# A fused attention and expert block on one core: the order of ScalarE and VectorE, in the loop and in the drain

## Chip, cores and metric

One core of one Trainium2 chip runs the whole program. The metric is the device time of one execution in microseconds (us). Its engines are TensorE (PE), VectorE (DVE), ScalarE (ACT), GpSimd (POOL) and SyncE (SP, which here only issues DMAs); each runs its own list of instructions in order and waits for the others by semaphores.

## What is computed

x has 16 images of 256 rows and 128 channels. Six rows of modulation per image come from a small matmul. Cut to what matters:

```python
h = layernorm(x) * (1 + ca) + sa
wave = silu(h @ wave_w.T + wave_b)           # 8 frequencies, 8 phases
freq, phase = mean(sigmoid(wave[0]) * 15 + 1), mean(tanh(wave[1]) * 16)
w = silu(h @ kernel_w.T + kernel_b)[..., :33]          # per head
pos = clip(l + (s - 16) * freq + phase, 0, 255)        # 33 places per row
out = sum_s w[s] * lerp(h, pos[s])                     # per head of 16 channels
x = x + ga * silu(out @ out_w.T)
h = layernorm(x) * (1 + cb) + sb
mask = one_hot(top_2(softmax(h @ router_w.T + router_b)))   # 8 experts
x = x + gb * (sum_e mask[e] * (h @ expert_w[e]) + mask @ expert_b)
```

## The kernel before

The 16 images are handled in nine units: image 0 alone, seven pairs, image 15 alone (`UNITS`, `LATE` is unit 7, `LAST` unit 8). An image is two tiles of 128 rows. The order of each engine is written out by hand as one loop over i, in which `run(i, lag, stage)` issues `stage` for unit i + lag, and `second` does so for the second image of a pair. So one iteration works on several units at once: the front of unit i + 1 (norm, transposes, projection rows, the line of positions), the middle of unit i (network, AT, A, attention), the back of unit i - 1 (sum with x, second norm, logits, the two best experts) and the experts of unit i - 2. What follows the loop is the drain.

The middle, on VectorE: `network` (L814, six stages of predicated copies that move the 33 weights of each row to their places in T, masks from `eI`), `spread_out` (L847, AT from T and the cells c, one instruction for each tile), `set_ends` (L857). `places` (L770) makes `eI` of unit i + 1 from uR, which ScalarE makes in `front_u` (L484, L491). On ScalarE, `front_c` (L502) and `front_fall` (L508, the Relu) make c, and `mid_A` (L519) copies A out of four PSUM banks, which TensorE fills with transposes (L1066, `mid_A`). `mid_attend` (L1080), `mid_y` (L1090) and `mid_gate` (L1096) end in pY.

The back: `residual` (L866, VectorE) adds pY to x and leaves row sums. ScalarE's `stats2` (`squares`, L380 and L383) and GpSimd's `rstd2` (L322, L328, L330) give the norm, `norm2` (L417) applies it, TensorE transposes xn (`back_x2T`, L1106), ScalarE makes h2T (`back_h2T`, L552), TensorE the logits (`back_logits`, L1117), VectorE `lg`, `top` and `hit` (L880 to L896), TensorE and ScalarE the mask rows mkT (`back_mk`, L1127 and L561). SyncE writes mkT to DRAM (L297) and reads it back to all partitions as mkb (L301, `masks`). In the next iteration VectorE's `masked` (L915) multiplies mkb and h2T into hm for each image, TensorE runs a plain part and seven experts for each image (`back_plain` L1167 and L1170, `back_experts` L1151), ScalarE scales (`back_moe`, L568), TensorE transposes back (L1177), and `total` (L920) adds to x. Units 7 and 8 spread their masks by TensorE instead (`back_mb`, L1139, read by `masked` at L909).

The sums for the first norm of unit i + 2 are `sums1` (L394), `squares1` (L383) and `norm1` (L417) on ScalarE, `rstd1` on GpSimd. `warm_up` (L1000) issues matmuls whose result nobody reads. ScalarE's order in the part of the loop that the change touches:

```python
run(i, 1, front_row, 2)
run(i, 0, front_fall)
run(i, 1, front_row, 3)
run(i, 1, front_wave)
...
run(i, -1, stats2)
...
run(i, 2, sums1)
run(i, 1, front_u)
run(i, -1, norm2)
...
run(i, 2, squares1)
run(i, -1, back_h2T)
run(i, -2, back_moe)
run(i, 0, mid_A, 0)
run(i, -1, back_mk)
```

## Time and profile before

| | |
|---|---|
| runs shown | 292.1, 292.21, 293.36 us; median 292.21 |
| the profiled execution | 291.6 us, its span 289.8 us |
| PE busy | 263.6 us (91%) |
| DVE busy | 259.2 us (89%) |
| ACT busy | 228.0 us (79%) |
| POOL busy | 40.2 us (14%) |
| network of unit 8 starts (end of the loop) | 242.71 us |

The span is the time from the first to the last instruction of the profiled execution. In the views below times are in us from the start of the span; a timeline row gives start, length and the instruction (line, operation, output from inputs, count), and in brackets how long the engine had been idle before it and what it waited for. Rows that start where the one before them still has its last tenth of a us overlap it. A table by stage has, for each engine, its busy time and the number of instructions, then the clock granted to TensorE (1.00 is 2.4 GHz, 0.50 is 1.2 GHz).

### The profile page before, as it was taken

The numbers are of one execution on the slowest core, as the hardware profiler recorded it, in microseconds if no ns is written. First come the engines' busy times: TensorE is split into PE (matmuls) and PEld (weight loads), VectorE is DVE, ScalarE is ACT, GpSimd is POOL, SyncE is SP. The second block draws the span as 40 slices with busy tenths as digits, with TensorE's granted clock in tenths as the row PEclk, the third lists the DMA queues.
The fourth block names the chain that finished last, engine by engine and source line by source line (L and its number), as shares of the span: only waits on it lengthen the run. The fifth ranks groups of instructions, "written<-read, shape, count | busy, mean of one in ns | idle before, by whom it ended". The sixth has DMA issues, their size and how long they took to land.

```text
span 289.8 us, 5448 instructions
## 1 busy us (share of the span) xinstructions
PE 263.6 (91%) x1884; PEld 182.7 (63%) x1884; DVE 259.2 (89%) x543; ACT 228.0 (79%) x641; POOL 40.2 (14%) x61
## 2 busy tenths in 40 slices
PE   7999886999889998999899998999999989999895
PEld 3444642874567476866587477837884778487664
DVE  7989999998969998999989998999999999973462
ACT  4885899599978998899979998899779767655310
POOL 4203402300410022000200012002400300040100
PEclk9999998699999999999999999999999999999999
DMA  6550000020002000050005000500041004100101
GB/s 180 195 129 0 0 0 0 2 66 1 1 0 119 31 1 0 3 163 3 0 1 165 0 0 2 160 8 1 2 104 62 1 0 118 49 2 0 38 0 54
DMA packets 11869, 12.08 MB, mean 42 GB/s; under 512 B 1014, under 2 KB 10818, under 8 KB 11842
## 3 DMA queue, kind: packets, MB, share of 16 engines
q1 hardware_dynamic: 11398, 11.33, 13.0%
q10 hardware_dynamic: 444, 0.40, 0.5%
q8 instruction: 15, 0.25, 0.3%
q14 instruction: 12, 0.10, 0.1%
HBM read 9.59 MB, written 2.14 MB: 40 GB/s over the span
## 4 chain that ended last, share of the span: by engine, by line
ACT 32%; DVE 31%; PE 24%; issue 11%; POOL 1%; ACTq 0%; DVEq 0%; POOLq 0%
DVE AT L847 13%; ACT A L519 6%; DVE T L814 5%; ACT xn L383 4%; PE pT L1066 4%; ACT xn L417 4%; ACT c L502 3%; PE pE L1151 3%; PE pY L1151 2%; PE pL L1117 2%; PE pR L1066 2%; ACT u L484 2%; ACT T L453 2%; ACT hT L440 2%; PE pR L1043 1%
## 5 line engine op out<-in xcount | busy, mean ns | idle before, releaser
L814 DVE COPY_PREDICATED T<-mask,T 128x1472 f32<-128x1472 int16 (+9 forms) x54 | 76.6, 1418 | 0.5
L847 DVE TENSOR_TENSOR AT<-T,c 128x2064 f32<-128x2064 f32 x32 | 72.4, 2305 | 0.0
L519 ACT ACTIVATE A<-pT 128x512 f32<-128x512 f32 x64 | 35.1, 603 | 27.6 <-PE pT L1066 27.0
L1151 PE MATMUL pE<-hm,late 128*128 128x256 f32 x196 | 47.0, 387 | 0.0
L1151 PEld LDWEIGHTS pE<-hm,late 128*128 128x128 f32 x196 | 35.8, 190 | 5.9
L1066 PE MATMUL pT<-first,AT 128*128 128x128 f32 x256 | 34.6, 279 | 3.2 <-DVE AT L857 3.1
L519 ACT ACTIVATE A<-pR 128x512 f32<-128x512 f32 x64 | 35.5, 622 | 0.3 <-PE pR L1066 0.3
L322 POOL TENSOR_SCALAR ve<-sq 128x4 f32<-128x4 f32 (+1 forms) x14 | 9.9, 710 | 185.3 <-ACT xn L383 185.3
L1066 PEld LDWEIGHTS pT<-first,AT 128*128 128x128 f32 x256 | 29.4, 144 | 9.2 <-DVE AT L857 7.7
L1066 PE MATMUL pR<-first,AT 128*128 128x128 f32 x256 | 33.9, 276 | 0.0
L1080 PE MATMUL pY<-A,hs 128*32 128x256 f32 x512 | 32.4, 383 | 0.3
L1066 PEld LDWEIGHTS pR<-first,AT 128*128 128x128 f32 x256 | 29.8, 144 | 0.0
L417 ACT ACTIVATE xn<-x,nm,rs 128x128 f32<-128x128 f32 x64 | 26.4, 483 | 2.2 <-POOL nm L330 2.2
L915 DVE TENSOR_TENSOR hm<-mkb,h2T 128x1792 f32<-128x1792 bf16 x13 | 26.2, 2017 | 1.2 <-POOL rs L328 1.2
L502 ACT ACTIVATE c<-near,early 128x172 f32<-128x172 f32 (+1 forms) x54 | 26.0, 569 | 0.0
L1043 PE MATMUL pR<-proj,hT 128*128 128x297 f32 x62 | 23.8, 465 | 0.9 <-ACT hT L440 0.9
L328 POOL TENSOR_TENSOR rs<-ve,mhalf 128x4 f32<-128x4 f32 (+1 forms) x18 | 17.4, 968 | 42.3 <-DVE ve L727 35.4
L1080 PEld LDWEIGHTS pY<-A,hs 128*32 128x32 f32 x512 | 16.9, 109 | 9.5 <-ACT A L519 4.9
L1000 PE MATMUL pE<-warm 128*128 128x512 bf16 x88 | 21.3, 400 | 1.2 <-DVE warm L655 1.2
L383 ACT ACTIVATE xn<-x,mu 128x128 f32<-128x128 f32 x52 | 20.2, 390 | 0.5
L1000 PE MATMUL pT<-warm 128*128 128x512 bf16 x65 | 18.1, 401 | 0.0
L1000 PEld LDWEIGHTS pE<-warm 128*128 128x128 bf16 x88 | 8.9, 103 | 11.5 <-issue 1.9
(153 smaller groups left out, 403.1 us busy)
## 6 DMA issues: line engine op xcount, KB each, us to landing
mkb<-mask_rows SPq DMA_DIRECT2D x6, 896.0 KB, 5.0
x<-in_x SPq DMA_DIRECT2D x7, 256.0 KB, 5.7
out<-x SPq DMA_DIRECT2D x7, 256.0 KB, 5.0
late<-in_late SPq DMA_DIRECT2D x1, 592.0 KB, 3.8
mkb<-mask_rows SPq DMA_DIRECT2D x1, 448.0 KB, 3.5
x<-in_x SPq DMA_DIRECT2D x2, 128.0 KB, 3.5
wmod<-in_wmod ACTq DMA_DIRECT2D x1, 256.0 KB, 4.4
out<-x SPq DMA_DIRECT2D x2, 128.0 KB, 3.2
```

Source lines behind the costliest of these rows:

```text
L383: ins = nc.scalar.activation(junk[:, bt, :], of_x(n)[:, bt, :], ACT.Square, bias=mu[:, bt:bt + 1], accum_out=sq[:, bt:bt + 1])
L417: ins = nc.scalar.activation(xn[:, bt, :], of_x(n)[:, bt, :], ACT.Identity, bias=nm[:, bt:bt + 1], scale=rs[:, bt:bt + 1])
L502: nc.scalar.activation(cells[:, :, :, r], near[:, 0:w, :], ACT.Abs, bias=off[:, r:r + 1]).then_inc(a_abs, 1)
L519: nc.scalar.activation(A[b][:, m, 2 * j:2 * j + 2, :].rearrange("p h l -> p (h l)"), four_banks(k)[:, :], ACT.Copy).then_inc(a_A, 1)
L814: nc.vector.copy_predicated(rows[:, :, :, j0:j1], spread(mask[:, k, 0:w, j0:j1], [P, w, H, j1 - j0], 2), rows[:, :, :, j0 + (1 << bit):j1 ...
L847: nc.vector.tensor_tensor(cells_of(bt).rearrange("p h (j r) -> p h j r", r=BLK), spread(T[n % 2][:, bt, 0:H, 0:NB], [P, H, NB, BLK], 3), s ...
L915: nc.vector.tensor_tensor(hm[b][:, :, :], mkb[n % 2][:, :, b * L:(b + 1) * L], spread(own, [P, EM, L], 1), ALU.mult).then_inc(v_hm, 1)
L1000: mm(bank[:, :], warm[:, 0:P], warm[:, :], start=True, stop=True)
L1043: mm(dst, hT[:, bt * P:(bt + 1) * P], proj[:, :], start=False, stop=True).then_inc(t_row, 1)
L1066: ins = nc.tensor.transpose(four_banks(k)[:, c0:c0 + P], AT[:, 2 * b + i, 2 * j + a, OVER + m * P:OVER + (m + 1) * P], ident)
L1080: ins = mm(pY[32 * j:32 * j + 32, b * L:(b + 1) * L], hs[n % 2][:, 2 * b + m, hh, :], A[b][:, m, hh, :], start=(m == 0 and a == 0), stop=( ...
L1151: ins = mm(dst, weT[:, e, :], hm[b][:, e, :], start=False, stop=(e == EM - 1))
```

## The change

ScalarE: `front_fall` moves behind `stats2`; `norm2` moves ahead of `sums1`, and `back_h2T` ahead of `front_u`. VectorE: from iteration 3 on the sum with x (`residual`) stands behind the second masked input; `selectors` moves to the end of iteration 0's network; `expert_weights` moves there from GpSimd, one iteration later; in the drain both masked inputs of unit 6 stand among the stages of unit 8's network. SyncE: the last mkb transfer is issued in two parts with a semaphore each. TensorE: `back_plain` covers both images in one pass; in iteration i the transposes of xn stand behind two of the seven experts of the second image; the four warm-ups behind them are issued in iterations 1 and 2 alone; in iteration 7 `back_mk(6)` stands between the halves of A; the drain runs unit 6's experts before unit 8's A.

```diff
@@ sync, masks(n)
-                sp.dma_start(mkb[n % 2][:, :, 0:w], spread(scratch[n % 2][:, 0:w], [P, EM, w], 0)).then_inc(d_mkb[n % 2], 16)
+                parts = ((0, L, d_mkb[n % 2]), (L, w, d_mkl)) if n == LATE - 1 else ((0, w, d_mkb[n % 2]),)
+                for c0, c1, landed in parts:
+                    sp.dma_start(mkb[n % 2][:, :, c0:c1],
+                                 spread(scratch[n % 2][:, c0:c1], [P, EM, c1 - c0], 0)).then_inc(landed, 16)
@@ gpsimd
-            def expert_weights():
-                pool.wait_ge(d_late, 32)
-                nc.gpsimd.tensor_tensor(weT[:, 0:EM, :], weT[:, 0:EM, :], spread(weT[:, EM, :], [P, EM, C], 1),
-                                        ALU.subtract).then_inc(g_we, 1)
-                pool.wait_ge(g_we, 1)
-                nc.gpsimd.tensor_scalar(weT[:, EM, :], weT[:, EM, :], 2.0, None, ALU.mult).then_inc(g_we, 1)
...
-                if i == 0:
-                    expert_weights()
@@ scalar, loop
                 run(i, 1, front_row, 2)
-                run(i, 0, front_fall)
                 run(i, 1, front_row, 3)
                 run(i, 1, front_wave)
...
                 run(i, -1, stats2)
+                run(i, 0, front_fall)
                 if i >= 0:
                     run(i, 1, front_hs)
+                run(i, -1, norm2)
                 run(i, 2, sums1)
+                run(i, -1, back_h2T)
                 run(i, 1, front_u)
-                run(i, -1, norm2)
...
                 run(i, 2, squares1)
-                run(i, -1, back_h2T)
                 run(i, -2, back_moe)
-                run(i, 0, mid_A, 0)
-                run(i, -1, back_mk)
+                run(i, 0, mid_A, 0, (0,))
+                if i == LATE:
+                    back_mk(LATE - 1)
+                run(i, 0, mid_A, 0, (1,))
+                if i < LATE:
+                    run(i, -1, back_mk)
@@ scalar, drain
             mid_gate(LATE)
+            back_moe(LATE - 1)
             mid_A(LAST, 0)
...
             back_mk(LATE)
-            back_moe(LATE - 1)
@@ vector
+            def expert_weights():
+                dve.wait_ge(d_late, 32)
+                (the two operations as above, on nc.vector, with v_we)
...
                 run(i, 0, network, range(4, 5))
-                run(i, -1, residual)
+                if i < 3:
+                    run(i, -1, residual)
                 second(i, -2, masked, 1)
+                if i >= 3:
+                    run(i, -1, residual)
                 run(i, 0, network, range(5, 6))
+                if i == 0:
+                    selectors()
+                elif i == 1:
+                    expert_weights()
@@ vector, drain
-            network(LAST, range(2, 6))
             masked(LATE - 1, 0)
+            network(LAST, range(2, 4))
+            masked(LATE - 1, 1)
+            network(LAST, range(4, 6))
...
             stats2(LATE)
-            dve.wait_ge(g_rs2, LATE + 1)
-            masked(LATE - 1, 1)
             route(LATE)
             residual(LAST)
             stats2(LAST)
+            total(LATE - 1)
             masked(LATE, 0)
-            total(LATE - 1)
@@ tensor
-                mm(dst, weT[:, EM, :], h2T_of(n)[:, b * L:(b + 1) * L], start=True, stop=False)
+                w = tiles(n) * P
+                mm(moe_bank(n)[:, 0:w], weT[:, EM, :], h2T_of(n)[:, 0:w], start=True, stop=False)
...
                 run(i, -2, back_experts, 0)
-                second(i, -2, back_experts, 1)
+                second(i, -2, back_experts, 1, range(0, 2))
...
                 run(i, -1, back_x2T)
-                if i > 0:
+                second(i, -2, back_experts, 1, range(2, EM))
+                if 0 < i < 3:
                     warm_up(4, pT[0])
...
+                if i == LATE:
+                    back_mk(LATE - 1)
                 run(i, 0, mid_A, 0, 1)
-                run(i, -1, back_mk)
+                if i < LATE:
+                    run(i, -1, back_mk)
@@ tensor, drain
-            warm_up(5, pT[0])
+            back_experts(LATE - 1, 0, range(0, 4))
             mid_y(LATE)
-            warm_up(6, pT[0])
-            back_experts(LATE - 1, 0, range(0, 2))
+            back_experts(LATE - 1, 0, range(4, EM))
             mid_gate(LATE)
-            back_experts(LATE - 1, 0, range(2, EM))
+            back_experts(LATE - 1, 1)
+            warm_up(8, pT[0])
             mid_A(LAST, 0, 0)
             mid_A(LAST, 0, 1)
+            back_out(LATE - 1)
...
             mid_gate(LAST)
-            back_experts(LATE - 1, 1, range(3, 6))
+            warm_up(4, pT[0])
             back_mk(LATE)
-            back_experts(LATE - 1, 1, range(6, EM))
             back_mb(LATE, 0)
-            back_out(LATE - 1)
             back_experts(LATE, 0, range(0, 4))
```

## Rows read from the trace of the kernel before

**Rows 1.** The page, busy time and share of the span.
```profile
PE 263.6 (91%) x1884; PEld 182.7 (63%) x1884; DVE 259.2 (89%) x543; ACT 228.0 (79%) x641; POOL 40.2 (14%) x61
```
**Rows 2.** Busy time by stage: iteration 5, iteration 7, the drain.
```profile
153.16:184.13 30.97, 28.66 (x221) 21.00 (x219) 29.81 (x57) 28.44 (x82) 3.13 (x6) 1.00 0.14 39
...
214.09:242.71 28.62, 26.72 (x211) 19.65 (x209) 28.38 (x58) 22.14 (x56) 2.22 (x3) 1.00 0.15 42
242.71:289.80 47.09, 42.72 (x294) 30.50 (x291) 28.59 (x79) 20.22 (x46) 3.93 (x4) 1.00 0.14 40
```
**Rows 3.** Timeline of VectorE, the waits in iterations 0, 2, 3 and 5.
```profile
20.87 0.22 DVE L735 TENSOR_REDUCE sums<-th 128x8 f32<-128x64 f32 x1 [0.70 <-ACT th L475]
...
83.73 0.19 DVE L880 TENSOR_TENSOR lg<-pL,rb 128x32 f32<-128x32 f32 x1 [2.83 <-PE pL L1117]
...
114.70 0.19 DVE L880 TENSOR_TENSOR lg<-pL,rb 128x32 f32<-128x32 f32 x1 [1.15 <-PE pL L1117]
...
176.64 0.19 DVE L880 TENSOR_TENSOR lg<-pL,rb 128x32 f32<-128x32 f32 x1 [0.92 <-PE pL L1117]
```
**Rows 4.** Timeline of VectorE, iteration 0 and one masked input of iteration 5.
```profile
29.79 2.27 DVE L801 TENSOR_TENSOR near<-sf,f 128x172 f32<-128x172 f32 x1
...
32.94 1.07 DVE L674 CAST sel<-first 24x896 bf16<-24x896 f32 x1
...
159.77 2.01 DVE L915 TENSOR_TENSOR hm<-mkb,h2T 128x1792 f32<-128x1792 bf16 x1
```
**Rows 5.** Timeline of GpSimd: the expert weights, and two last steps of a norm.
```profile
29.77 2.09 POOL L356 TENSOR_TENSOR late<-late 128x896 f32<-128x896 f32 x1
...
76.89 1.33 POOL L330 TENSOR_TENSOR nm<-mu,rs 128x4 f32<-128x4 f32 x1
...
200.62 0.77 POOL L330 TENSOR_TENSOR nm<-mu,rs 128x4 f32<-128x4 f32 x1
```
**Rows 6.** Timeline of TensorE and VectorE in iteration 1: y's transposes, the sum with x.
```profile
39.52 0.44 PE L1096 MATMUL pY<-first,y 128*128 128x128 f32 x2 [0.36 <-ACT y L541]
...
42.27 0.27 DVE L866 SCALAR_TENSOR_TENSOR x<-pY,x 128x128 f32<-128x128 f32 x1
```
**Rows 7.** Timeline of TensorE: pauses for xn, experts of an image, hT's transposes.
```profile
48.33 0.44 PE L1106 MATMUL pX<-first,xn 128*128 128x128 f32 x2 [2.19 <-ACT xn L417]
...
79.95 0.66 PE L1106 MATMUL pX<-first,xn 128*128 128x128 f32 x4 [1.50 <-ACT xn L417]
...
165.81 3.29 PE L1151 MATMUL pE<-hm,late 128*128 128x256 f32 x14
...
223.52 0.38 PE L1049 MATMUL pX<-first,hT 128*128 128x128 f32 x2
```
**Rows 8.** Busy time and granted clock behind the pause at 46 us.
```profile
49.00:55.00 6.00, 5.83 (x23) 4.04 (x22) 6.00 (x16) 2.70 (x9) 2.84 (x3) 0.50 0.01 3
```
**Rows 9.** Timeline of ScalarE in iteration 5: Relu, stats2, sums1, u, norm2, h2T.
```profile
164.23 1.05 ACT L508 ACTIVATE c<-c 128x1032 f32<-128x1032 f32 x1
...
166.07 0.19 ACT L380 ACTIVATE mu<-sum 128x4 f32<-128x4 f32 x1
...
168.32 0.30 ACT L394 ACTIVATE xn<-x 128x128 f32<-128x128 f32 x1
...
169.49 1.38 ACT L484 ACTIVATE u<-early,nlf,invf 128x50 f32<-128x50 f32 x4
...
171.18 1.63 ACT L417 ACTIVATE xn<-x,nm,rs 128x128 f32<-128x128 f32 x4
...
174.49 1.00 ACT L552 ACTIVATE h2T<-pX,modT 128x256 f32<-128x256 f32 x2
```
**Rows 10.** Timeline of VectorE: AT in iteration 2, prodN in iteration 6.
```profile
75.86 4.52 DVE L847 TENSOR_TENSOR AT<-T,c 128x2064 f32<-128x2064 f32 x2
...
200.53 0.79 DVE L825 TENSOR_TENSOR prodN<-T,kap 128x608 f32<-128x608 f32 x1
```
**Rows 11.** The page, DMA issues: count, KB each, median us to landing.
```profile
mkb<-mask_rows SPq DMA_DIRECT2D x6, 896.0 KB, 5.0
```

50 lines of the change are left out of this document (26 added, 24 removed).

## Prediction

> **What bounds the kernel now.** The page first: VectorE and TensorE are both busy for about nine tenths of the span, ScalarE for four fifths [rows 1]. Busy time by stage comes next. In a full iteration of the loop (153.16 to 184.13) VectorE works 29.81 of 30.97 us, ScalarE 28.44 and TensorE 28.66: VectorE leads, and ScalarE has some 2.5 us of room. In the drain VectorE is busy for 30.5 of 47.1 us and TensorE for 42.7 [rows 2]. So the loop goes by VectorE, the drain by TensorE. The timeline of VectorE then shows where it stands still in the loop: 0.70 us in iteration 0 for the tanh of the next unit, and at the logits 2.83, 1.15, 0.92 (two such) us in iterations 2 to 5 [rows 3]. Those waits, 5.8 us in all, are what the new order of ScalarE can win.
>
> I write T for the start of an iteration's network: 153.16 for iteration 5 [rows 2], so its 176.64 is T+23.5.
>
> **The start: expert weights and selectors.** Removed from GpSimd: two instructions. The first, 2.09 us long, started 0.02 us before VectorE's `near`, which took 2.27 us where its sisters take about 0.34 [rows 4, 5]; removing it gives back 1.93 us. They come to VectorE as a product-like operation of 896 elements (half of the 1792 that take 2.01 us, so 1.0 us [rows 4]) and a small one of some 0.2 us: +1.2 us, nothing beside it to hide it. The selectors (1.07 us [rows 4]) only move; they now stand where VectorE waited 0.70 us, so that wait goes: -0.7. But everything behind them in iteration 0, AT's first half too, is 0.3 us later, and with it the chain through A, y and its transposes (39.52 to 39.96), while the sum with x (42.27) would come 2.6 us earlier, at 39.6 [rows 6]. It then waits until 40.3: +0.65. Net at the end of iteration 1: -0.7 - 1.93 + 1.2 + 0.65 = **-0.8 us**.
>
> **Iteration 1, TensorE's pause.** Before, TensorE paused 2.19 us for xn, and right after it the granted clock stood at 0.50, the 1.2 GHz level, for 6 us and more [rows 7, 8]. In the new order xn(0) is ready about 1.7 us earlier (norm2 ahead of sums1 and u), while the 18 warm-ups still run, so that pause goes. What TensorE has after it (four and two warm-ups, four logits matmuls) ends near 48.9, and A's transposes can't start before VectorE's first ends, about 51.4. The pause is 2.5 us and lies later: the low clock would now fall on both halves of A and on the attention. With no low clock the next chain starts as soon as AT is there, and iteration 2 ends 1.3 us earlier than before; with the low stretch of before (6.8 us, half of it lost) it ends 1.3 us later. I take half such a stretch, since the work behind this pause is dense: **-0.4 us** at the start of iteration 3, ends -1.3 and +1.3.
>
> **Iteration 2.** Here ScalarE is the bound before and after. stats2 comes 1.0 us earlier, since the Relu (1.05 us [rows 9]) stands behind it; norm2, sums1, h2T and then u follow. GpSimd's last step ran into AT: 1.33 us against its usual 0.20, ending with the AT instruction [rows 5, 10]. It does so again, so norm2 starts at AT's first end in any case. The logits are 1.4 us earlier, but u is now behind h2T and `places` (eI from uR), which stands before the logits on VectorE and before the ends that release A, waits 3.4 us instead. So the 2.83 us become a wait in another place, and only what the chain gained is left; that is inside the -0.4.
>
> **Iterations 3 to 5.** The sum with x stands behind the second masked input (2.01 us, 1.94 from start to start) and ends at T+13.0. ScalarE, which started stats2 at T+12.9 [rows 9], is there earlier, now that the Relu is behind, but waits for the sum: stats2 at T+13.1, ending T+14.9. GpSimd needs three steps, the last at T+16.5. VectorE's prodN starts at T+16.4. In iteration 6 of before the same order of starts (200.62 behind 200.53) cost it 0.77 us instead of 0.20 [rows 5, 10]. The Trainium skill, "SBUF — State Buffer", section "SBUF: two separate sides", says that GpSimd and VectorE share a pair of ports as an exclusive lock, held for a whole instruction. By that rule the step waits in every iteration from three on, as the row has it. So norm2 starts at T+17.35 and ends T+18.9 (its four take 1.63 us, the last 0.09 beside the next); sums1 takes 1.17, h2T 0.9, u with uR 1.69 [rows 9]: uR at T+22.7. VectorE asks for it at T+21.95: a wait of 0.75. TensorE, with 14 passes of 3.29 us for each half [rows 7] and two of seven experts ahead of xn's transposes, has the logits at T+22.7, ahead of the question. The question for the logits moves from T+22.55 to T+23.25, against T+23.7, T+23.5 and T+23.5 of before [rows 3]: **-1.0 us** for the three. Iteration 6 had no wait; with two tiles less in sums1 the new one is 0.3: **+0.3**.
>
> What is queued behind the new waits: `set_ends` and the second half of AT on VectorE; behind stats2 on ScalarE the Relu, done at T+15.9, which AT doesn't need before prodN and prodF are done, past T+17. mkT comes 1.0 us later against T, and mkb's transfer (5.0 us at the median [rows 11]) lands at about T+5.3, 1.3 us ahead of its first reader; one slow transfer of 6.6 us would cost 0.5. The four warm-ups removed, and `back_plain` in one pass of 512 columns instead of two of 256, save TensorE 1.2 us an iteration, beside other work: nothing.
>
> **Iteration 7.** The next unit has one image, so TensorE is at the experts 2.3 us sooner in the iteration (hT's transposes at T+9.4 [rows 7], T being 214.09 [rows 2]). Plain part 1.2, first half 3.1, two experts 0.9: done at 229.2. xn(6) comes from the sum (now 227.1), 1.8 of stats2, 1.8 of GpSimd, 1.5 of norm2: 232.4. The other five experts (2.2 us) and the logits come after it: logits at 236.25, asked for at 235.7. VectorE waits 0.55 and TensorE enters the drain 0.8 later: **+0.8 us**.
>
> **The drain.** TensorE's work is nearly the same: 12 warm-ups instead of 11 (+0.2), three double passes merged (-0.7). New pauses: before the logits of unit 7 (0.6, no expert work is left to fill it), before its masks (0.9 in two); gone: 0.7 at the masks, where ScalarE's copy waited for the experts. VectorE has the masked inputs 3 us ahead of TensorE. AT of the last unit comes 2.4 us later but 2 us before TensorE is free of the experts and 8 warm-ups. Splitting mkb's transfer adds one issue, with slack. Sum: **-0.1 us**.
>
> **Sum.** -0.4 - 1.0 + 0.3 + 0.8 - 0.1 = -0.4 us. The profiled execution took 291.6 us (span 289.8 and 1.8 around it), so 291.2; the median of the runs is 0.6 above the profiled one, which gives 291.8.
>
> **Rivals.**
> *A. The low clock in iteration 7 (slower).* The pause of TensorE between the second expert and xn's transposes is 3.2 us there. A pause of 2.19 was followed by the low clock, one of 1.50 was not [rows 7, 8]. If it decides, ten us of unbroken TensorE work behind it run partly at 1.2 GHz, and the drain behind them is TensorE's too, so each microsecond lost counts: 1.7 us for half a stretch, 3.4 for a whole one. That is 293.5 to 295.2. For it: the length. Against: dense matmuls on both sides of the pause, where before, warm-ups with gaps and tiny matmuls followed. Chance 0.29; it decides above about 2 us of pause.
> *B. No low clock anywhere and GpSimd gets in ahead of prodN (faster).* 0.1 us earlier is enough for that. Then norm2 starts 0.7 earlier, the waits for uR and the logits vanish in iterations 3 to 6 (-3.0 in place of -0.7) and the start keeps -1.3; iteration 7 loses 0.5: -1.3 - 3.0 + 0.5 - 0.1 = -3.9, or 288.3. For it: in iterations 3 to 5 of before VectorE lost 3.0 us at the logits, and 1 us less in front of them is in reach. Against: the sum with x is itself 1.9 us later. Chance 0.27.
> *C. The forecast*, new waits about as long as the old: 0.44.
>
> **Range and chances.** 289.0 leaves out the best half of B; 294.9 takes in most of A. A measurement of this kernel tells 0.5% (1.5 us) from no change, so faster is below 290.75: most of B and the lower edge of C (only the better end of iteration 1 moves it there), 0.35. Slower is above 293.67: most of A, 0.23. Same: 0.42.
>
> **What the profile would show.** Right: `near` in iteration 0 at 0.34 us; no wait for th in iteration 0; VectorE waiting for ScalarE's uR at `places`, 3 us in iteration 2 and under 1 in 3 to 5, and hardly at the logits; GpSimd's last step at 0.7 us or more; an idle TensorE before xn's transposes, 1.5 us in 3 to 6 and 3 in 7; a drain of 47 us. Wrong: no wait at `places`; a granted clock of 0.5 anywhere behind iteration 3; a masked input waiting for mkb; or a drain more than 1 us longer or shorter.

## The result: slower by 3.8%, and the profile after

The changed kernel took 303.95 us in the median of six runs (301.88 to 307.56), the kernel before 292.15 us in its six beside them (291.55 to 293.46). The ratio is **1.038, interval 1.033 to 1.043**. The forecast was 291.8 in a range of 289.0 to 294.9; the result lies 9 us above the range. Executions over 1.5% longer than the shortest one of the same kernel, like the one of 307.56 us, count in no ratio. The profiled execution took 304.53 us with a span of 302.70.

The page of the changed kernel, its busy line and two costly groups (GpSimd's, and the norm on ScalarE with its idle time and what ended it):

```profile
PE 265.7 (88%) x1844; PEld 181.9 (60%) x1844; DVE 258.8 (86%) x545; ACT 228.9 (76%) x641; POOL 65.7 (22%) x59
...
L332 POOL TENSOR_TENSOR rs<-ve,mhalf 128x4 f32<-128x4 f32 (+1 forms) x18 | 33.8, 1879 | 48.6 <-DVE ve L733 41.8
L410 ACT ACTIVATE xn<-x,nm,rs 128x128 f32<-128x128 f32 x64 | 26.7, 490 | 21.8 <-POOL nm L334 21.8
```

Against [rows 1] VectorE, ScalarE and TensorE did as much as before. GpSimd is the one that changed: 65.7 us instead of 40.2, with fewer instructions, and ScalarE waited 21.8 us for GpSimd's last step of a norm. In the page of before those two groups stood like this:

```profile
L417 ACT ACTIVATE xn<-x,nm,rs 128x128 f32<-128x128 f32 x64 | 26.4, 483 | 2.2 <-POOL nm L330 2.2
...
L328 POOL TENSOR_TENSOR rs<-ve,mhalf 128x4 f32<-128x4 f32 (+1 forms) x18 | 17.4, 968 | 42.3 <-DVE ve L727 35.4
```

The same 18 steps of four numbers per partition (the power -1/2) took 968 ns each before and 1879 ns after. Nothing in the change touches them. Busy time by stage, as [rows 2], for iterations 4, 5, 7 and the drain:

```profile
125.06:158.41 33.35, 28.61 (x213) 19.66 (x212) 29.80 (x58) 28.25 (x82) 9.92 (x7) 1.00 0.12 37
158.41:192.78 34.37, 29.51 (x213) 21.44 (x212) 29.90 (x57) 28.95 (x84) 10.17 (x8) 0.95 0.11 35
...
223.23:253.82 30.59, 26.53 (x200) 19.31 (x199) 28.53 (x57) 22.60 (x58) 1.43 (x3) 0.94 0.16 48
253.82:302.70 48.88, 42.90 (x291) 30.43 (x290) 28.40 (x79) 20.20 (x46) 2.10 (x4) 1.00 0.12 34
```

VectorE works 29.8 us in a full iteration as before; the iteration lasts 33.35 us instead of 30.97. The fifth number pair is GpSimd: 9.92 us instead of 3.13. The granted clock (the third number from the right) was 1.00 there, so it is not TensorE's clock that makes iteration 4 longer. So the time went into waits. The list of VectorE's waits names them (us in total, times, the longest), first of the changed kernel, then of before, which has no wait for uR:

```profile
DVE eI L776 <- ACT uR L484: 14.0, 6, 3.5
DVE lg L886 <- PE pL L1132: 11.0, 3, 8.7
```
```profile
DVE lg L880 <- PE pL L1117: 10.9, 5, 5.1
```

The 8.7 and the 5.1 us stand in the drain. In the loop the waits for the logits did shrink, from 5.8 to 2.3 us, as the change meant them to.

The starts of the iterations, read as T was read in the prediction (the first network stage on VectorE's timeline), give a table that every run below is compared by (profiled executions, us):

| kernel | start of it. 2 | it. 2 | it. 3 to 5 | it. 6 | it. 7 | drain |
|---|---|---|---|---|---|---|
| before | 58.66 | 32.30 | 93.17 | 29.96 | 28.62 | 47.09 |
| changed | 57.88 | 33.76 | 101.14 | 30.45 | 30.59 | 48.88 |
| difference | -0.78 | +1.46 | **+7.97** | +0.49 | +1.97 | +1.79 |

The differences add up to 12.9 us, the growth of the span (302.7 - 289.8). Eight of them lie in three iterations that the forecast had at -1.0. Iteration 5 is 1.0 us longer than iteration 4 and has a granted clock of 0.95 in the table by stage, some 3.4 us at the 1.2 GHz level; that part may be the clock's.

**How an iteration loses 2.4 us.** First GpSimd's timeline, from iteration 3 into 4 of the changed kernel. Steps ve, rs, nm come in threes; the first three are those of the first norm of unit i+2, the others (their ve is left out) of the second norm of unit i-1, one iteration on.

```profile
118.92 0.19 POOL L326 TENSOR_SCALAR ve<-sq 128x4 f32<-128x4 f32 x1 [7.37 <-ACT xn L376]
119.19 6.13 POOL L332 TENSOR_TENSOR rs<-ve,mhalf 128x4 f32<-128x4 f32 x1
125.40 0.21 POOL L334 TENSOR_TENSOR nm<-mu,rs 128x4 f32<-128x4 f32 x1
...
141.62 1.46 POOL L332 TENSOR_TENSOR rs<-ve,mhalf 128x4 f32<-128x4 f32 x1
143.16 1.74 POOL L334 TENSOR_TENSOR nm<-mu,rs 128x4 f32<-128x4 f32 x1
```

Then VectorE's timeline over the same time:

```profile
117.02 0.37 DVE L776 SCALAR_TENSOR_TENSOR eI<-uR,early 128x200 int16<-128x200 f32 x1 [3.31 <-ACT uR L484]
...
119.16 0.31 DVE L798 SCALAR_TENSOR_TENSOR sf<-sc,u 128x172 f32<-128x172 f32 x1
119.40 0.35 DVE L902 TENSOR_TENSOR hit<-late,topi 128x192 bf16<-128x192 f32 x1
119.67 4.51 DVE L853 TENSOR_TENSOR AT<-T,c 128x2064 f32<-128x2064 f32 x2
124.10 0.33 DVE L807 TENSOR_TENSOR near<-sf,f 128x172 f32<-128x172 f32 x1
124.35 0.21 DVE L863 COPY AT<-endw 128x32 f32<-128x32 f32 x1
```

And ScalarE's, which stands behind both:

```profile
125.73 1.65 ACT L410 ACTIVATE xn<-x,nm,rs 128x128 f32<-128x128 f32 x4 [1.97 <-POOL nm L334]
...
139.32 0.19 ACT L373 ACTIVATE mu<-sum 128x4 f32<-128x4 f32 x1
...
144.93 1.65 ACT L410 ACTIVATE xn<-x,nm,rs 128x128 f32<-128x128 f32 x4 [2.31 <-POOL nm L334]
```

1. The power step is asked for at 119.19, 0.03 us behind the start of sf. It is recorded until 125.32. Its unheld length is 1.01 us, so its own work began at about 124.31, as near gave way to the copy of the ends. All of VectorE's instructions between 119.16 and that point read two operands in SBUF.
2. The first norm of the next unit waits 1.97 us for it on ScalarE, in the next iteration, and everything behind it there is late: stats2 starts at T+14.26 (139.32 - 125.06). The sum with x had ended at T+13.0 (138.05), as forecast.
3. The second norm's steps therefore come a microsecond later than the forecast had them and meet prodN (141.42) and the first half of AT (142.54 to about 144.8). norm2 starts at T+19.87, not T+17.35; uR is 2.5 us late, and VectorE waits 3.31 us at `places`, not 0.75.
4. VectorE's later half of the iteration moves, but ScalarE's squares1 moves too, and asks for the power step 0.03 us behind sf again: 152.54 6.13 us in iteration 4. The loop holds itself there.

Before, the first norm's steps were asked for at T+21.6 (174.75), as VectorE's first pair of AT ended (175.20). Behind it VectorE ran small instructions or stood, and the steps took 0.51, 1.01 and 0.20 us:

```profile
174.75 0.51 POOL L322 TENSOR_SCALAR ve<-sq 128x4 f32<-128x4 f32 x1 [5.07 <-ACT xn L383]
175.33 1.01 POOL L328 TENSOR_TENSOR rs<-ve,mhalf 128x4 f32<-128x4 f32 x1
176.42 0.20 POOL L330 TENSOR_TENSOR nm<-mu,rs 128x4 f32<-128x4 f32 x1
```

squares1 then stood ahead of h2T; the change put it last, behind norm2, sums1, h2T and u, at T+27.

### The profile page after: what moved, and what is told of

Read it like the earlier page. It is cut to its first block, busy times and chain, and to the rows that moved or that the text cites. A ratio compares the mean times of both kernels' runs of the same rounds, so it can differ in the third digit from the quotient of the medians.

```text
span 302.7 us, 5384 instructions
## 1 busy us (share of the span) xinstructions
PE 265.7 (88%) x1844; PEld 181.9 (60%) x1844; DVE 258.8 (86%) x545; ACT 228.9 (76%) x641; POOL 65.7 (22%) x59
## 4 chain that ended last, share of the span: by engine, by line
ACT 34%; PE 23%; DVE 17%; POOL 14%; issue 10%; ACTq 0%; POOLq 0%; DVEq 0%
POOL rs L332 9%; ACT A L512 9%; ACT xn L410 6%; ACT xn L376 5%; POOL nm L334 4%; DVE T L820 4%; PE pE L1168 4%; DVE AT L853 4%; PE pT L1081 3%; ACT c L495 3%; PE pR L1058 2%; PE pY L1168 2%; ACT u L477 2%; ACT y L534 2%; PE pR L1081 2%
## 5 line engine op out<-in xcount | busy, mean ns | idle before, releaser
L1168 PE MATMUL pE<-hm,late 128*128 128x256 f32 x196 | 48.1, 397 | 0.0
L332 POOL TENSOR_TENSOR rs<-ve,mhalf 128x4 f32<-128x4 f32 (+1 forms) x18 | 33.8, 1879 | 48.6 <-DVE ve L733 41.8
L410 ACT ACTIVATE xn<-x,nm,rs 128x128 f32<-128x128 f32 x64 | 26.7, 490 | 21.8 <-POOL nm L334 21.8
L326 POOL TENSOR_SCALAR ve<-sq 128x4 f32<-128x4 f32 (+1 forms) x14 | 5.9, 421 | 167.8 <-ACT xn L376 167.8
L1168 PEld LDWEIGHTS pE<-hm,late 128*128 128x128 f32 x196 | 37.9, 200 | 7.0 <-issue 1.8
L1081 PE MATMUL pT<-first,AT 128*128 128x128 f32 x256 | 37.1, 291 | 5.2 <-DVE AT L863 5.0
L1081 PEld LDWEIGHTS pT<-first,AT 128*128 128x128 f32 x256 | 30.3, 149 | 12.6 <-DVE AT L863 10.4
L1081 PE MATMUL pR<-first,AT 128*128 128x128 f32 x256 | 35.7, 285 | 0.0
L334 POOL TENSOR_TENSOR nm<-mu,rs 128x4 f32<-128x4 f32 (+1 forms) x18 | 23.8, 1321 | 1.4
L1095 PEld LDWEIGHTS pY<-A,hs 128*32 128x32 f32 x512 | 15.9, 109 | 12.4 <-ACT A L512 7.4
L1015 PE MATMUL pE<-warm 128*128 128x512 bf16 x88 | 21.8, 405 | 1.2 <-DVE warm L652 1.2
L1121 PE MATMUL pX<-first,xn 128*128 128x128 f32 x32 | 6.3, 324 | 13.6 <-ACT xn L410 13.5
```

The costliest lines, as they stand in the source:

```text
L332: nc.gpsimd.tensor_tensor(rs[:, 0:w], ve[:, 0:w], mhalf[:, 0:w], ALU.pow).then_inc(out, 1)
L334: nc.gpsimd.tensor_tensor(nm[:, 0:w], mu[:, 0:w], rs[:, 0:w], ALU.mult).then_inc(last, 1)
L410: ins = nc.scalar.activation(xn[:, bt, :], of_x(n)[:, bt, :], ACT.Identity, bias=nm[:, bt:bt + 1], scale=rs[:, bt:bt + 1])
L1081: ins = nc.tensor.transpose(four_banks(k)[:, c0:c0 + P], AT[:, 2 * b + i, 2 * j + a, OVER + m * P:OVER + (m + 1) * P], ident)
L1095: ins = mm(pY[32 * j:32 * j + 32, b * L:(b + 1) * L], hs[n % 2][:, 2 * b + m, hh, :], A[b][:, m, hh, :], start=(m == 0 and a == 0), stop=( ...
L1168: ins = mm(moe_bank(n)[:, b * L:(b + 1) * L], weT[:, e, :], hm[b][:, e, :], start=False, stop=(e == EM - 1 and b == UNITS[n][1] - 1))
```

## The experiments

### Which part of the change costs what

**Runs e6 and e7**: the kernel before with one part of the change each.

```diff
# e6: ScalarE's loop order alone (stats2, Relu, hs, norm2, sums1, h2T, u, squares1)
# e7: the sum with x behind the second masked input from iteration 3 on, alone
-                run(i, -1, residual)
+                if i < 3:
+                    run(i, -1, residual)
                 second(i, -2, masked, 1)
+                if i >= 3:
+                    run(i, -1, residual)
```

> The kernel before with ScalarE's new order in the loop alone (Relu behind stats2, norm2 ahead of sums1, h2T ahead of u, squares1 last). Theory L2 (squares1 now ends so late that GpSimd's steps of the first norm meet the second pair of AT instructions and end after both, so the next iteration's xn is late on ScalarE): the pow step takes 6 us in iterations 2 to 5, periods rise to 31.5 us or more, and the kernel is 1 to 3% slower than before although the sum with x has not moved: 295 to 300 us. Rival M (only the moved sum does harm, the order alone wins the logits' waits): 287 to 290 us.

> The kernel before with the sum with x behind the second masked input from iteration three on, nothing else. By now theory L2 says that the first norm's steps on GpSimd decide and the second norm's hardly: ScalarE has u ahead of norm2 here, norm2 starts at T+18.0, and GpSimd's last step ends by T+17.3 even if held off by prodN. So no change: 291 to 293 us, wait at the logits 1.0 to 1.4 us in iterations 3 to 5. Theory L as first stated (the moved sum decides) expects at least 2 us more per iteration, 298 or above.

e6: 300.28 us, ratio **1.032 (1.028 to 1.036)**. e7: 292.38 us, 1.001 (0.998 to 1.004). ScalarE's order alone makes most of the loss; the later sum alone is worth nothing in the whole (its iterations 3 to 5 took 94.5 us against 93.2, its iteration 2 0.6 us less). GpSimd's timeline of e6 shows why, and which of the two norms does it:

```profile
117.51 6.12 POOL L328 TENSOR_TENSOR rs<-ve,mhalf 128x4 f32<-128x4 f32 x1
...
139.98 1.01 POOL L328 TENSOR_TENSOR rs<-ve,mhalf 128x4 f32<-128x4 f32 x1
141.06 0.20 POOL L330 TENSOR_TENSOR nm<-mu,rs 128x4 f32<-128x4 f32 x1
```

The second norm's steps are as quick as they can be. The first norm's power step takes 6.1 us, and iterations 2 to 6 last 31.8, 33.0, 32.7, 32.7 and 32.7 us.

**Runs e1 and e2**: the changed kernel with one part undone each (e1 ScalarE's old loop order, e2 the sum with x first in every iteration).

```diff
# e1, ScalarE
                 run(i, 1, front_row, 2)
+                run(i, 0, front_fall)
...
                 run(i, -1, stats2)
-                run(i, 0, front_fall)
...
-                run(i, -1, norm2)
                 run(i, 2, sums1)
-                run(i, -1, back_h2T)
                 run(i, 1, front_u)
+                run(i, -1, norm2)
...
                 run(i, 2, squares1)
+                run(i, -1, back_h2T)
# e2, VectorE
-                if i < 3:
-                    run(i, -1, residual)
+                run(i, -1, residual)
                 second(i, -2, masked, 1)
-                if i >= 3:
-                    run(i, -1, residual)
```

> The changed kernel with ScalarE's old order in the loop (the Relu ahead of the last row, u ahead of norm2, h2T behind squares1); all else as changed. Theory L (GpSimd's last step of the second norm is held off by VectorE's long two-input instructions, because the sum with x now comes 1.9 us later): norm2 still can't start before AT's first instruction ends, so the loss stays and only moves from the wait for uR to the logits: 300 to 305 us, 2 to 3 us of wait at the logits in iterations 3 to 5. Rival O (the new order itself costs it: u stands behind norm2, sums1 and h2T whatever GpSimd does): the loss goes, 291 to 294 us.

> The changed kernel with the sum with x ahead of the second masked input in every iteration. Theory L: stats2 ends a microsecond or more sooner, GpSimd's last step starts ahead of prodN and takes 0.2 us; the wait for uR in iterations 3 to 5 falls from 3.3 us to under 0.5 and the time to 291 to 296 us. Rival O: the sum is not what decides; the waits for uR stay above 2 us and the time at 300 us or more.

e1: 298.08 us, 1.018 (1.013 to 1.024). With the old order no power step of the loop took over 1.43 us from iteration 1 on; iterations 3 to 5 took 95.1 us. VectorE waited for the logits in their place, 19.0 us in eight, 8.7 of them in the drain. Most of what is left of e1's loss lies in the drain (49.5 us), in iteration 7 (30.8) and in iteration 5 (32.7), each with 3.4 us at the lower clock in it. e2: 295.62 to 301.43 us in four runs, 1.018 (1.009 to 1.026); in its profiled execution, of 301.36 us, iterations 3 to 5 took 94.5 us. By these ratios both kernels came out between what the theory and what the rival had expected. In e2 the second norm's last step took 0.20 us and the wait of over 3 us at `places` stood once instead of four times, yet the power step of the first norm still took 6.13 us in iterations 2 to 5 and VectorE waited 7.9 us at the sum with x. The two parts don't add up: to undo either takes some 6 us off the changed kernel, yet the first alone costs 8.5 us (300.28 against 291.76) and the second none. That they feed each other on GpSimd, as points 2 and 3 above have it, is argued and not shown: in e1 no step of a norm was held by more than 0.5 us in iterations 3 to 5.

### Is it GpSimd's reading?

**Run e4**: the changed kernel, in which each of GpSimd's three steps of a norm writes a constant and reads nothing. It leaves out the norms' scale and shift. **Run e5**: the same in the kernel before.

```diff
-                nc.gpsimd.tensor_tensor(rs[:, 0:w], ve[:, 0:w], mhalf[:, 0:w], ALU.pow).then_inc(out, 1)
+                nc.gpsimd.memset(rs[:, 0:w], 1.0).then_inc(out, 1)
```

> The changed kernel with GpSimd's three steps of each norm replaced by fills with a constant (the norms' scale and shift are left out, so the numbers differ): GpSimd reads nothing and finishes at once, all waits and orders stay. Theory L: no step can be held off; iterations 3 to 5 lose their waits for uR, and the late start of the first norm's xn goes too: 287 to 293 us. Rival O: GpSimd's own 1.5 us are saved, no more; 3 iterations of 3.3 us wait become 3 of about 2: 298 us or more.

> The kernel before with the same fills in place of GpSimd's three steps, as the control of the run above (the norms' scale and shift are left out). Theory L: here the steps ran mostly in free slots, so little is to be had: 1 to 3 us below the kernel before, 289 to 291. Rival O expects the same gain here as in the changed kernel (some 3 to 5 us in both).

e4: 288.66 us, **0.989 (0.985 to 0.992)**, 15 us below the changed kernel. Iterations 3 to 5 took 90.2 us, VectorE all but unbroken, and the waits at `places` came to 1.6 us. e5: 294.12 us, 1.004 (1.000 to 1.008); its iterations 3 to 5 took 93.2 us, as before. So the change to ScalarE's order does carry the gain that was looked for, even more (1.0 us an iteration, not 0.3), and GpSimd's steps take it away, and 2.7 us an iteration more. Before, they cost nothing. The gain expected of e5 was wrong: its loop was bound otherwise, and its iteration 2 started 2.9 us later (61.60 against 58.66), for a reason that was not followed up.

The fills differ from the steps in two ways: they read nothing, and they are shorter (0.10 us each). That the reading matters for the hold is seen in e5: three fills asked for inside AT's second half (51.73 to 54.0) went through at once, at 53.58, 53.74 and 53.90, 0.10 us each. How much of e4's 15 us is owed to the shorter length alone is not separated.

### What the steps wait for

**Run e8**: u ahead of norm2 on ScalarE, h2T and squares1 behind, the sum with x first. **Run e12**: the changed kernel with VectorE's final sum (which reads PSUM) moved between the second pair of AT.

```diff
# e8, ScalarE (the sum as in e2)          # e12, VectorE
+                run(i, 1, front_u)                        second(i, 0, spread_out, 2)
                 run(i, -1, norm2)       +                run(i, -2, total)
                 run(i, 2, sums1)                          second(i, 0, spread_out, 3)
                 run(i, -1, back_h2T)                      run(i, 1, cells_from)
-                run(i, 1, front_u)                        second(i, 0, set_ends, 1)
                 run(i, 2, squares1)     -                run(i, -2, total)
```

> The changed kernel with the sum with x first in every iteration and u ahead of norm2 on ScalarE (Relu still behind stats2; then u, norm2, sums1, h2T, squares1). Theory L2: the second norm's last step starts near T+15.4, ahead of prodN, and squares1 ends near T+22.3, so the first norm's steps end by T+24.1, ahead of the second AT pair (T+24.65): no step over 1.5 us, periods of iterations 3 to 6 at 29.9 to 30.3 us, 286 to 290 us. Rival O (it is ScalarE's load, not GpSimd's place): the periods stay above 31 us and the time above 294.

> The changed kernel with one call moved on VectorE: `total` (the sum of pE and x, one operand in PSUM) between the two instructions of the second AT pair instead of behind them. Theory L2: GpSimd's pow step, held off from the two-input instructions ahead of the pair until behind `near`, can get in at `total`: its 6.13 us fall to about 4, xn of the first norm no longer waits, and with it ScalarE's whole next iteration comes 2 us sooner; the wait for uR falls from 3.3 to about 1 us: 294 to 299 us. Rival S (GpSimd is held off by the length of one instruction only, and the pair's place is no matter): no change, 302 to 305 us.

e8: 293.53 us, 1.007 (1.004 to 1.010); iterations 3 to 5 took 93.0 us, so this order, with the sum first, takes all of the 8 us back. The 286 to 290 us of its theory were missed, since the periods stayed at 30.9 us or more. The power step gets through, but the next one doesn't. VectorE and GpSimd in e8:

```profile
145.90 0.35 DVE L902 TENSOR_TENSOR hit<-late,topi 128x192 bf16<-128x192 f32 x1
146.17 4.52 DVE L853 TENSOR_TENSOR AT<-T,c 128x2064 f32<-128x2064 f32 x2
150.60 0.33 DVE L807 TENSOR_TENSOR near<-sf,f 128x172 f32<-128x172 f32 x1
```
```profile
145.06 1.01 POOL L332 TENSOR_TENSOR rs<-ve,mhalf 128x4 f32<-128x4 f32 x1
146.14 4.88 POOL L334 TENSOR_TENSOR nm<-mu,rs 128x4 f32<-128x4 f32 x1
```

nm is asked for 0.03 us ahead of AT, during hit, and is held through both halves of AT and near. Neither the change from hit to AT nor that from the first half to the second lets it in.

e12: 297.39 us, 1.016 (1.009 to 1.023); iterations 3 to 5 took 93.5 us instead of 101.1. Its VectorE and GpSimd:

```profile
147.34 2.31 DVE L853 TENSOR_TENSOR AT<-T,c 128x2064 f32<-128x2064 f32 x1
149.55 0.69 DVE L928 TENSOR_TENSOR x<-pE,x 128x512 f32<-128x512 f32 x1
```
```profile
146.87 3.64 POOL L332 TENSOR_TENSOR rs<-ve,mhalf 128x4 f32<-128x4 f32 x1
150.59 2.20 POOL L334 TENSOR_TENSOR nm<-mu,rs 128x4 f32<-128x4 f32 x1
```

The power step now ends at 150.51, so its 1.01 us began at 149.50, where the final sum starts; before, it had to wait for near's end. Moving one instruction of VectorE that reads PSUM moved the release with it. This is the most direct reading of the mechanism, and it took 7.6 us out of three iterations. No run put an instruction with two SBUF operands in that place, so that it is the PSUM operand that lets GpSimd in rests on this one kind of instruction.

### The drain

**Run e9**: e8 with the drain of before. **Run e10**: the changed kernel with the drain of before. In both, TensorE's, ScalarE's and VectorE's order behind the loop, the transfer of mkb in one part and the order of masks and A in iteration 7 are the old ones; back_plain stays in one pass.

> As e8_u_and_sum_first, with the drain of the kernel before on all engines (mask rows of unit 6 behind A, one mkb transfer). The stretch from unit 8's network to the end was 48.67 and 48.88 us with the new drain against 47.09 us of before. If the new drain costs that by itself: 1.6 us less than e8 (284 to 288 us), stretch 47.0 to 47.3. If it only looks longer because the loop hands over later: the same time as e8 within 0.5 us. Either way the fastest version so far.

> The changed kernel with the drain of the kernel before, the loop as changed. If the new drain costs 1.7 us by itself: 302 us. If not: 304 us. By both theories of the loop the waits for uR in iterations 2 to 5 stay at 3.3 us.

e9: 292.02 us, 1.001 (0.998 to 1.003), drain 46.51 us against 48.79 in e8. e10: 301.03 us, 1.030 (1.026 to 1.033), drain 46.52 against 48.88. The new drain costs 2.3 us with either loop. The expectation of a gain for e9 failed: it only came level with before.

**Runs e15 and e16** take the new drain apart, with the changed kernel's loop: e15 without the 8 warm-ups ahead of the last unit's A, e16 with unit 6's second masked input and all that follows from it back at their old places, and without the change's two groups of warm-ups (8 and 4).

```diff
# e15, TensorE                            # e16, VectorE
             back_experts(LATE - 1, 1)                 network(LAST, range(2, 4))
-            warm_up(8, pT[0])           -            masked(LATE - 1, 1)
             mid_A(LAST, 0, 0)           ...
                                          +            masked(LATE - 1, 1)
                                                       route(LATE)
```

> The changed kernel without the 8 warm-up matmuls of the drain that stand between the experts of unit 6 and the last unit's A. In the changed kernel AT's last ends were written at 268.49 and the experts ended at 269.1, but A's first transpose started at 270.68. Theory (the warm-ups and the masked input ahead of AT are both on the path): A starts 1.6 us earlier and the drain takes 47.3 instead of 48.9 us. Rival (the warm-ups cost nothing, since the pause of TensorE would only move in front of the logits of unit 7, or the clock falls without them): drain 48.6 or more.

> The changed kernel with unit 6's second masked input, its experts, its copy and its final sum at their places of before; the first masked input stays ahead of the network, and back_plain stays in one pass. Theory (the second masked input ahead of AT is the drain's loss: it filled a wait for the second norm before, and delays AT by its 2.0 us now): AT of the last unit ends 1.9 us earlier against T(8) than in the changed kernel (T+12.8 instead of T+14.7), the logits of unit 7 come at T+22.5 to T+23.5 instead of T+26.0, and the drain takes 46.4 to 47.2 us. Rival (TensorE's experts are the drain's bound wherever VectorE's masked input stands): drain 48 or more.

One run each: e15 took 301.91 us with a drain of 48.97, e16 300.42 with 47.11. VectorE in the drain, first of the changed kernel, then of e16:

```profile
256.10 2.02 DVE L923 TENSOR_TENSOR hm<-mkb,h2T 128x1792 f32<-128x1792 bf16 x1 [0.69 <-DMA mkb<-mask_rows]
...
268.49 0.20 DVE L863 COPY AT<-endw 128x32 f32<-128x32 f32 x1
...
279.82 0.19 DVE L886 TENSOR_TENSOR lg<-pL,rb 128x32 f32<-128x32 f32 x1 [8.71 <-PE pL L1132]
```
```profile
264.40 0.20 DVE L863 COPY AT<-endw 128x32 f32<-128x32 f32 x1
266.92 2.02 DVE L923 TENSOR_TENSOR hm<-mkb,h2T 128x1792 f32<-128x1792 bf16 x1
...
274.73 0.19 DVE L886 TENSOR_TENSOR lg<-pL,rb 128x32 f32<-128x32 f32 x1 [5.80 <-PE pL L1132]
```

From the start of the drain (253.82 and 251.49) AT is ready after 14.7 us in the one and 12.9 in the other, unit 7's logits after 26.0 and 23.2. The second masked input stood in a wait of VectorE before. Ahead of AT it is on the path, and so is what stands ahead of A on TensorE, its experts and the 8 warm-ups; together they carry 1.8 of the 2.4 us, each from one execution. Of e15, the logits came after 24.6 us (275.69 - 251.13), 1.4 us sooner, as its theory had it, but the clock took that back. Busy time and granted clock of e15 from there on:

```profile
275.00:281.00 6.00, 4.78 (x28) 2.41 (x29) 5.13 (x28) 1.82 (x4) 0.89 (x2) 0.89 0.12 35
281.00:287.00 6.00, 6.00 (x28) 4.32 (x28) 1.09 (x4) 0.56 (x1) 0.00 (x0) 0.83 0.03 9
```

Some 3.4 us there ran at the 1.2 GHz level ((0.11 + 0.17) x 6 us, twice), where the changed kernel had 1.00 throughout its drain. Both the theory and the rival of e15 were partly right. That the missing warm-ups caused the fall is not shown: e1, e2 and e12 have all 8 of them, and in their drains (49.5, 50.4 and 49.9 us) 3.4 us ran at the 1.2 GHz level too, from 273.3, 279.2 and 271.7 us on.

### Towards a faster version

**Run e11**: e9 with the final sum between AT's second pair. **Run e13**: the kernel before with the expert weights and selectors on VectorE and the same move. **Run e14**: e11 with norm2 ahead of u and h2T ahead of sums1. **Run e17**: e14 with sums1 ahead of norm2.

```diff
# ScalarE in the loop, e17 against e11 (e14 is the step between)
                 run(i, 1, front_hs)
-                run(i, 1, front_u)
-                run(i, -1, norm2)
                 run(i, 2, sums1)
+                run(i, -1, norm2)
+                run(i, 1, front_u)
                 run(i, -1, back_h2T)
                 run(i, 2, squares1)
```

> e9_u_and_sum_first_old_drain with the same call moved between the AT pair. There GpSimd's last step started 0.03 us ahead of the pair and took 4.88 us, and ScalarE waited 1.5 us for it in each iteration. Theory L2: it gets in at `total`, norm1 is not held off, the logits come ahead of the question: periods of iterations 3 to 6 at 29.9 to 30.2 us instead of 30.9, 286 to 289 us, 1 to 2% below the kernel before. Rival S: 291 to 293 us as e9.

> The kernel before with two parts of the change or its like that should help by themselves: expert weights and selectors on VectorE as in the change, and `total` between the second AT pair. Theory L2: the start gives 0.8 us (unit 2's network at 57.9 instead of 58.7), and `total` gives nothing, since GpSimd's steps were free there: 290.5 to 291.5 us. Rival S the same.

> The kernel of e11 (sum with x first, the final sum between AT's second pair, drain of before) with two steps of ScalarE exchanged: the second norm ahead of u, and h2T ahead of sums1. In e11 the second norm's scales were there at T+16.1 (169.19), but its norm started at 170.47 behind u, and VectorE waited 0.58 to 0.9 us per iteration for the logits. Theory (logits chain is what is left of the loss): norm2 starts 1.2 us earlier, the logits come over 1 us earlier, the wait for them goes, uR is ready 0.3 us later and still ahead of its reader; iterations 3 to 7 take 30.0 to 30.3 us instead of 30.9, the span is 286 to 287 us and the ratio 0.98 to 0.99. Rival (GpSimd's steps behind VectorE's pair of products): ScalarE now asks for the second norm's last step sooner, and where prodN has started the step takes 0.7 us or more as in the changed kernel; norm2 then starts as late as in e11 plus 0.4, u behind it, and VectorE waits at places: 30.9 us an iteration as before, ratio 0.997 or more.

> The kernel of e14 with sums1 ahead of the second norm on ScalarE instead of behind h2T. In e14 GpSimd asked for the first norm's first step at 177.77, 0.06 us ahead of sf, and finished its third at 183.78; ScalarE then waited 1.28 us for it at the next norm, and VectorE 0.75 us at the sum with x of the next iteration. ScalarE also stood still for 0.34 us ahead of the second norm. Theory (the first norm's steps, held through VectorE's run of sf, hit and AT, set the period): sums1 fills the 0.34 us, squares1 ends 0.3 us earlier against T, the first step gets in ahead of sf, the power step too, and only the third is held until the final sum, so that all three are done by T+27.2 instead of T+30.05; the wait ahead of norm1 and the one at the sum with x go, and iterations 3 to 7 take 30.0 to 30.3 us, the ratio 0.98 to 0.99. Rival (a ring of ScalarE and TensorE sets the period whatever GpSimd does): the steps are quick, but VectorE waits as long in another place, and the iterations take 30.8 us as in e14, ratio 0.995 or more.

| kernel | median us | ratio (interval) | start of it. 2 | it. 2 | it. 3 to 5 | it. 6 | it. 7 | drain |
|---|---|---|---|---|---|---|---|---|
| e11 | 292.27 | 0.997 (0.994 to 1.000) | 58.25 | 32.34 | 92.70 | 30.90 | 28.84 | 47.17 |
| e13 | 295.89 | 1.010 (1.007 to 1.014) | 58.44 | 33.10 | 95.27 | 30.54 | 28.68 | 47.67 |
| e14 | 291.69 | 0.999 (0.997 to 1.002) | 57.89 | 33.28 | 92.56 | 30.83 | 28.67 | 47.17 |
| e17 | 290.79 | **0.997 (0.995 to 0.998)** | 59.36 | 31.98 | 91.26 | 30.22 | 28.68 | 47.10 |

e11 missed. The last step of the first norm was held for 2.4 us instead of 4.9, up to the final sum, as its theory had it, and ScalarE's waits for GpSimd fell from 10.2 to 2.3 us; but the periods stayed at 30.9 us, so that hold was not what set them. e14 missed too. Its wait for the logits went, and VectorE waited 0.75 us at the sum with x instead: squares1 ended 0.06 us ahead of sf, the first norm's steps were held once more, and the chain behind norm1 was late. GpSimd in iteration 5 of e14:

```profile
177.77 2.91 POOL L322 TENSOR_SCALAR ve<-sq 128x4 f32<-128x4 f32 x1 [7.51 <-ACT xn L372]
...
181.85 1.93 POOL L330 TENSOR_TENSOR nm<-mu,rs 128x4 f32<-128x4 f32 x1
```

e17 asks 1.2 us earlier against T (T+23.7 instead of T+24.9; its theory had 0.3), and two of the three get through:

```profile
175.89 0.19 POOL L322 TENSOR_SCALAR ve<-sq 128x4 f32<-128x4 f32 x1 [6.93 <-ACT xn L372]
176.16 1.01 POOL L328 TENSOR_TENSOR rs<-ve,mhalf 128x4 f32<-128x4 f32 x1
177.25 2.34 POOL L330 TENSOR_TENSOR nm<-mu,rs 128x4 f32<-128x4 f32 x1
```

All three are done by T+27.4 (179.59 - 152.18) instead of T+30.9, the wait at the sum with x is gone, and iterations 3 to 5 take 30.42 us each instead of 30.85. That is the sign that the theory gave, at 0.4 us of the 0.6 to 0.9 it promised, so its ratio of 0.98 to 0.99 was missed too. Of the kernels that leave nothing out, e17 is the one that is faster than the kernel before by more than its interval, by 0.35%. In e13 the first norm's steps were quick, as the old order has them, and it lost all the same, where 290.5 to 291.5 us had been expected. It waited 12.8 us for the logits in seven (before: 10.9 in five), and 3.4 us of its iteration 4 ran at the 1.2 GHz level, which no part of that iteration did before; what else made it slow stays open.

## Why the prediction was wrong

**The step that failed** is the one headed "Iterations 3 to 5", forecast at -1.0 us and measured at +8.0, of which some 1.0 in iteration 5 may be the clock's. It followed the second norm's chain and its three steps on GpSimd, and for the first norm's three steps, which squares1 sets off, it had no price. The prediction moved squares1 to the end of ScalarE's round and never asked where its GpSimd steps would then fall. They fell into VectorE's run sf, hit, AT, AT, near, and took 6.7 us from the first's start to the third's end (118.92 to 125.61) instead of 1.9. Runs e6 (the order alone: +8.5 us), e12 (the step let in earlier: 7.6 us less in the three iterations) and e4 (steps that read nothing: -15 us) show it.

**Inside that step** the other numbers held where they didn't hang on it. The sum with x ended at T+13.0, as forecast. That the second norm's last step meets VectorE's products was right in kind. Its price was 0.57 us in the forecast and 1.54 us here (1.74 - 0.20), because it came 1.6 us later, into AT. The Trainium skill, "SBUF — State Buffer", section "SBUF: two separate sides", gives the rule of a lock between the two engines, which was used there. The trace agrees that a step is held, yet not in the size: a lock that is held for one instruction would have let the step of e8 in behind hit or behind AT's first half, and it waited for both halves and near.

**The start**: right. Iteration 2 was forecast to start 0.8 us earlier, and did (57.88 against 58.66). Its parts held as well, so this was not luck: `near` took 0.34 us, the wait for th went, the expert weights took 1.3 us of VectorE against 1.2, and the sum with x waited 0.51 us against 0.65.

**Iterations 1 and 2**: iteration 3 was forecast 0.4 us earlier, ends -1.3 and +1.3, and came 0.7 later. TensorE's pause was where it was expected, and the low clock came with it whole, not by half. The ends have their middle at 0 and not at -0.4, so the forecast's own half stretch was priced too low:

```profile
51.41 1.97 PE L1081 MATMUL pT<-first,AT 128*128 128x128 f32 x8 [2.26 <-DVE AT L863]
```
```profile
46.00:52.00 6.00, 3.23 (x17) 1.72 (x16) 6.00 (x9) 5.37 (x24) 0.41 (x1) 0.85 0.00 0
52.00:58.00 6.00, 6.00 (x38) 5.83 (x40) 6.00 (x14) 4.13 (x8) 5.77 (x3) 0.58 0.01 3
```

(0.15 + 0.42) x 6 us, twice, is 6.8 us at the lower level, as much as in the kernel before. `places` waited 3.30 us in iteration 2, forecast 3.4.

**Iteration 6**: +0.49 against +0.3. **Iteration 7**: +1.97 against +0.8. TensorE's pause ahead of xn's transposes was 3.36 us, forecast 3.2, and behind it rival A's low clock came at its smaller size:

```profile
241.65 1.12 PE L1121 MATMUL pX<-first,xn 128*128 128x128 f32 x4 [3.36 <-ACT xn L410]
```
```profile
238.00:244.00 6.00, 2.64 (x10) 2.08 (x9) 5.79 (x14) 4.23 (x11) 1.43 (x3) 0.78 0.01 3
244.00:250.00 6.00, 6.00 (x47) 5.22 (x46) 4.18 (x21) 3.66 (x10) 0.00 (x0) 0.94 0.00 0
```

That is 3.4 us at the lower level, 1.7 lost. The wait for the logits was 1.54 us against 0.55. Over all kernels here the length of iteration 7 goes with that clock: in the eight profiled executions that had a stretch of it there (the changed kernel, e1, e2, e8, e10, e12, e15, e16) it took 30.4 to 31.6 us, in the ten others 28.6 to 29.1, among them e4 (28.58), which has all of the changed order. So 1.7 of the 1.97 us are most likely the clock's. The pause alone doesn't decide. e8 and e9 stood still for nearly the same time ahead of xn's transposes (3.02 us up to 231.47 and 3.09 us up to 231.53); e8's granted clock in iteration 7 was 0.94 and it took 30.42 us, e9's was 1.00 and it took 28.81. What does decide was not found.

**The drain**: +1.79 against -0.1. The forecast's own terms add up to +0.3 (0.2 - 0.7 + 0.6 + 0.9 - 0.7), not to -0.1. TensorE's work was 42.90 us against 42.72 [rows 2], where the forecast had 0.5 us less; AT of the last unit was 2 us ahead of TensorE, as forecast (268.7 against 270.7). The term that was mis-sized most is that of the pauses: TensorE stood still for 6.0 us (48.88 - 42.90) where it had 4.4, and the forecast had some 0.8 us of new pauses. In the program's order, the experts and warm-ups ahead of A delay A, ScalarE has unit 7's norm behind A's copies, and the experts that used to fill the pauses behind it were spent; of this, e16 shows the first part (1.8 us). The first masked input waited another 0.69 us for mkb, which the forecast had seen only for the loop. The masked input that had filled VectorE's wait was taken as moved for nothing, though its cover stayed behind.

**The rivals.** A named a slower end by the clock in iteration 7: the mechanism came, at its smaller size of 1.7 of the 12.9 us, but not by its condition. Pauses of 2.36 and 2.56 us in iterations 3 and 4 of the changed kernel, and e9's of 3.09, had no low clock with them, so its border of about 2 us does not hold. B asked for GpSimd to get in ahead of prodN. In e2 and e6 it did (0.20 us), and the kernels were slow all the same, so B rested on the same gap. No rival had the first norm.

**The signs.** `near`, th, the 3 us at `places` in iteration 2 and GpSimd's last step at 0.7 us or more came as the prediction said. The wait at `places` in iterations 3 to 5 was 3.3 to 3.5 us and not under 1, TensorE's pause ahead of xn's transposes there 2.4 to 2.6 us and not 1.5, and three of the signs of being wrong came: a granted clock of 0.5 behind iteration 3 (iterations 5 and 7), a masked input waiting for mkb (0.69 us in the drain), and a drain over 1 us longer.

## What to carry to other kernels

When a step is moved, follow what it sets off on the other engines, not only who waits for its own result: here a step of ScalarE had a shadow of three tiny instructions on GpSimd, and their place against VectorE's long run decided the loop. A group whose mean time doubles while its shape stays the same is the first thing to look at in a profile after. Where such steps can't be taken off GpSimd, have them asked for ahead of VectorE's unbroken run, or put an instruction that reads PSUM into the middle of the run. The second pays only where the hold is on the path: it took 6 us off in e12 and nothing in e11.

## What the runs showed of the hardware

A GpSimd instruction on four numbers per partition took 0.20 us (a product) or 1.01 us (a power) alone, and up to 4.88 and 6.13 us (a product on two numbers, at 217.49 in the changed kernel, 5.19) when asked for as a run of VectorE instructions with two SBUF operands was starting or under way. What counts is whether the step has begun: a power step that had begun before such a run (176.16 in e17, sf at 176.72) took its 1.01 us. VectorE's own instructions took no longer beside it (sf 0.32 us). The large product of the expert weights (128x896, 2.09 us) was another matter: `near`, 0.02 us behind it, took 2.27 us instead of 0.34 [rows 4, 5]. A fill, which reads nothing, took 0.10 us inside AT (e5). The hold ended at an instruction with an operand in PSUM (e12, e14, e17) or with one operand (the copy, changed kernel and e8).

Not every change between two such instructions kept GpSimd out. In iteration 4 of the changed kernel the power step asked for at 141.62, during prodN, ended at 143.08, so it began at about 142.07, as prodN gave way to prodF, and nm got in between AT's first two halves. Between hit and AT, and between the two halves of AT that stand behind hit, it never did. What makes the difference is open, and no run separates it.

Where a step falls seems to turn on a microsecond elsewhere. With the same loop code, e15's iterations 3 to 5 took 34.50, 30.73 and 34.38 us, the changed kernel's 33.42, 33.35 and 34.37. Each of the three over 34 us has 3.4 us at the 1.2 GHz level in it. In e15's iteration 3 the power step was asked for ahead of the run (118.46) and took 1.01 us, nm behind it 4.88, and the iteration behind them took 30.73 us.
